# Two adaLN transformer layers: the softmax shifts turned by one transpose, and written by four transfers a unit

## The reference, cut to what matters

```
scores = jnp.einsum('bhqd,bhkd->bhqk', q, k) / jnp.sqrt(jnp.float32(HEAD_DIM))
scores = jnp.where(causal[None, None], scores, -jnp.inf)
attn = jax.nn.softmax(scores, axis=-1)
out = jnp.einsum('bhqk,bhkd->bhqd', attn, v)
```

## Time and profile before

| | us |
|---|---|
| median of 3 runs | 1355.31 (1354.32 to 1356.49) |
| span of the profiled execution | 1351.6 |
| PE busy | 1152.9 |
| DVE busy | 962.7 |
| ACT busy | 695.5 |
| POOL busy | 240.5 |

### The profile page before, as it was taken

One profiled execution on the slowest core, in us unless ns is written; L12 is line 12 of the kernel. 1 busy time (PEld: TensorE's weight loads), 2 busy tenths in 40 slices (PEclk: granted clock), 3 DMA queues, 4 the chain that ended last, 5 costly groups with the idle time before them and its releaser, 6 DMA issues. The chain is left out here.

```text
span 1351.6 us, 39302 instructions
## 1 busy us (share of the span) xinstructions
PE 1152.9 (85%) x16626; PEld 581.8 (43%) x16627; DVE 962.7 (71%) x2700; ACT 695.5 (51%) x929; POOL 240.5 (18%) x271
## 2 busy tenths in 40 slices
PE   5878999999899997297368899999899999778993
PEld 4423434434344444175123343444334454546662
DVE  5888989989698853511558998989788882564553
ACT  4424657666567674142334465766666668323330
POOL 2440000101000000277121000100200000135761
PEclk9678989999899997599678898999999999689997
DMA  4441000503200000221353111330400000011123
GB/s 142 142 80 41 19 19 19 92 19 55 57 3 5 5 3 2 45 54 53 95 154 65 35 37 36 67 65 4 76 3 4 5 4 3 1 40 38 48 47 107
DMA packets 38022, 60.46 MB, mean 45 GB/s; under 512 B 6288, under 2 KB 29104, under 8 KB 36720
## 3 DMA queue, kind: packets, MB, share of 16 engines
q0 software_dynamic: 7648, 24.47, 9.2%
q1 hardware_dynamic: 30208, 33.57, 8.6%
HBM read 42.84 MB, written 14.12 MB: 42 GB/s over the span
## 5 line engine op out<-in xcount | busy, mean ns | idle before, releaser
L978 ACT ACTIVATE probs_at<-st 128x1024 f32<-128x1024 f32 (+3 forms) x640 | 545.1, 897 | 323.2 <-PE st L931 221.1
L996 DVE TENSOR_REDUCE mxp_at<-mx 128x1 f32<-128x512 f32 x768 | 497.3, 685 | 69.1 <-PE mx L898 67.6
L898 PE MATMUL mx<-ks,qs 128*32 128x512 bf16 (+3 forms) x5120 | 390.8, 367 | 40.5 <-DVE mxp_at L996 11.4
L931 PE MATMUL st<-qs,ks 128*32 128x512 bf16 (+3 forms) x5120 | 363.5, 355 | 10.6 <-DMA qs<-shrow_at 8.1
L949 PE MATMUL av<-probs_at,vs 128*32 128x512 f32 (+3 forms) x2560 | 290.9, 530 | 0.3
L898 PEld LDWEIGHTS mx<-ks,qs 128*32 128x32 bf16 x5120 | 137.2, 97 | 344.3 <-DVE mxp_at L996 140.6
L998 DVE CUSTOM_DVE_ANT_0 junk_at<-mx,maskN 128x384 f32<-128x384 f32 (+3 forms) x512 | 240.9, 485 | 39.3 <-PE mx L898 36.2
L931 PEld LDWEIGHTS st<-qs,ks 128*32 128x32 bf16 x5120 | 133.9, 98 | 97.8 <-ACT probs_at L978 22.6
L1274 POOL DMA_INDIRECT taken<-table,token x71 | 68.1, 959 | 251.1 <-DVEq L1063 218.3
L935 PE MATMUL st<-maskTb,identb 128*32 128x128 bf16 x2048 | 103.8, 220 | 0.0
L949 PEld LDWEIGHTS av<-probs_at,vs 128*32 128x32 f32 x2560 | 69.7, 111 | 47.8 <-issue 5.6
(11 more groups left out here) (271 smaller groups left out, 1043.5 us busy)
## 6 DMA issues: line engine op xcount, KB each, us to landing
qs<-q_parts POOLq DMA_DIRECT2D x54, 128.0 KB, 5.7
ks<-k_parts POOLq DMA_DIRECT2D x18, 384.0 KB, 6.7
weights<-in_w_dram SPq DMA_DIRECT2D x16, 256.0 KB, 3.0
table<-rows SPq DMA_DIRECT2D x8, 260.0 KB, 5.4
got_pj<-eo SPq DMA_DIRECT2D x4, 512.0 KB, 5.5
got_cb<-eo SPq DMA_DIRECT2D x4, 512.0 KB, 5.4
weights<-in_dw_dram SPq DMA_DIRECT2D x3, 576.0 KB, 4.9
weights<-in_gw_dram SPq DMA_DIRECT2D x3, 528.0 KB, 3.8
```

The lines of the kernel that those rows point to most:

```text
L898: mm = pe.matmul(buf[z:z + 32, 0:w], QS[p][:, j, (4 * Q + qb) * P + z:(4 * Q + qb) * P + z + 32], KS[p][:, j, c * CH:c * CH + w], start=Tr ...
L931: mm = pe.matmul(st[half][z:z + 32, y, off:CH], KS[p][:, j, kb * P + z:kb * P + z + 32], QS[p][:, j, Q * CH + off:(Q + 1) * CH], start=Tru ...
L978: act.activation(probs[:, s % 2, 2 * half:2 * half + 2, off:CH], st[half][:, :, off:CH], ACT.Exp, scale=SCALE).then_inc(exp_done[half], 1)
L996: ins = v.tensor_reduce(dst, buf[:, 0:w], AX.X, ALU.max)
```

## The change

The four blocks of a unit's shifts are turned by a single transpose, 128x32 to 32x128: row 8 * block + r. The copy takes 32 rows of 128 columns. As the blocks now lie under one another and not side by side, each goes to its place by a transfer of its own, 8 rows x 4 heads x 128 columns; the semaphores count four. The planner's two costs of a turn change with it.

```diff
@@ schedule()
             else:
-                pe += .22
-                dve = max(dve, pe + lat) + .6
+                pe += .06
+                dve = max(dve, pe + lat) + .25
                 ready[x] = dve + 2.4
@@ attention()
-        shrow = sb("shrow", [2 * GH, 4, CH], BF)
+        shrow = sb("shrow", [TPC * 2 * GH, 4, P], BF)
@@ SyncE
                         sp.wait_ge(shift_row, UB + u + 1)
-                        sp.dma_start(QS[g % 2][SHIFT0:SHIFT0 + 2 * GH, :, Q * CH:(Q + 1) * CH],
-                                     shrow[:, u % 4, :].unsqueeze(1).to_broadcast([2 * GH, GH, CH])).then_inc(shift_set[u % 4], 16)
+                        for qb in range(TPC):
+                            b = TPC * Q + qb
+                            sp.dma_start(QS[g % 2][SHIFT0:SHIFT0 + 2 * GH, :, b * P:(b + 1) * P],
+                                         shrow[2 * GH * qb:2 * GH * (qb + 1), u % 4, :].unsqueeze(1).to_broadcast([2 * GH, GH, P])
+                                         ).then_inc(shift_set[u % 4], 16)
@@ GpSimd
-                g.wait_ge(shift_set[0], 16 * (L * (NU // 4) + 1))
+                g.wait_ge(shift_set[0], 16 * TPC * (L * (NU // 4) + 1))
@@ TensorE
                         pe.wait_ge(shift_split, UB + x + 1)
-                        for qb in range(TPC):
-                            mm = pe.transpose(buf[:].bitcast(BF)[0:2 * GH, qb * P:(qb + 1) * P], nsh[:, x % 4, qb, :], m.identb[:])
-                        mm.then_inc(mx_ready, 1)
+                        pe.transpose(buf[:].bitcast(BF)[0:TPC * 2 * GH, 0:P], nsh[:, x % 4].rearrange("p q r -> p (q r)"),
+                                     m.identb[:]).then_inc(mx_ready, 1)
@@
-                            pe.wait_ge(shift_set[u % 4], 16 * (L * (NU // 4) + u // 4 + 1))
+                            pe.wait_ge(shift_set[u % 4], 16 * TPC * (L * (NU // 4) + u // 4 + 1))
@@ VectorE
                         if x >= 4:
-                            v.wait_ge(shift_set[x % 4], 16 * (L * (NU // 4) + x // 4))
-                        v.tensor_copy(shrow[:, x % 4, :], buf[:].bitcast(BF)[0:2 * GH, 0:CH]).then_inc(shift_row, 1)
+                            v.wait_ge(shift_set[x % 4], 16 * TPC * (L * (NU // 4) + x // 4))
+                        v.tensor_copy(shrow[:, x % 4, :], buf[:].bitcast(BF)[0:TPC * 2 * GH, 0:P]).then_inc(shift_row, 1)
```

## The result

The changed kernel takes 1393.7 us (median of 4 runs, 1393.06 to 1395.03) against 1354.8 for the one before beside it: ratio 1.0299, 95% interval 1.0266 to 1.0332. I forecast slower, 1368.6 us, with a range up to 1378: the sign was right, the size a third of the real one. The profiled execution has a span of 1392.5 us against 1351.6, 40.9 more.

A forecast was written before the change was run, and what follows sets the result against it. TensorE and VectorE, handing three PSUM banks to and fro, bound the attention stages. 22.2 us more wait x 0.86 = 19.1 lost, less 5.8 won on the copy: 13.3 us slower, 1368.6 us, range 1354 to 1378.

The forecast's parts named there:

- The copy: VectorE's shift copy on 32x128 takes 0.19 us; 6.8 us of VectorE saved, 5.8 us of time won.
- The issues: SyncE issues each of a unit's four shift transfers in about 0.69 us, the last 2.19 us later than the only one now.
- cheap issues: Rival: back-to-back SyncE issues cost 0.34 us each, as on L739; 2.3 us slower, 1357.6 us; chance 0.18.
- The landing in a quiet queue: At uncontended gates the last shift transfer lands 2.46 us after its issue, which comes 2.19 us later than now.
- the nine: Units without a DMA wait now, scores 2.47 to 3.19 us after the issue; 17.2 us more wait.
- Which gates: Scores of 14 units would wait for shift transfers: nine with little slack and five already waiting.
- The contended five: Units where TensorE already waits for the DMA, 9.9 us together; 5 us more wait, between 0 and 11.0.
- How much arrives: Comparing the two attention layers, 0.86 of a TensorE wait reaches the end; 22.2 us of wait loses 19.1 us.
- the banks that cover the gates: Rival: VectorE's three filled banks, 1.8 us of work, cover TensorE's gate waits; 4 us faster, 1351.5 us; chance 0.1.
- Fixed costs in a row: Rival: each shift transfer lands before the next moves, 7.4 us at each of 14 gates; +81 us, 1436 us; chance 0.02.
- The planner's costs: Turn costs of 0.06 and 0.25, not 0.22 and 0.6, leave gates tight; order elsewhere worth 3 us either way.
- the rival 'order': Rewritten order puts more products ahead of the gates, 6 to 9 us faster, 1347 us, or fewer, slower; chance 0.1.

The follow-up runs named there:

- the two by two: Changed kernel with the planner's old or new turn costs for first/last eight units: old/old 1380.9, new/old 1387.1, old/new 1384.8, new/new 1391.5 us.

## Why the prediction was wrong

- *The copy*: predicted 0.19 us, measured 0.205; DVE busy 954.2 us against 962.7. Right. What it is worth in time was 5.8 us in my sum. Transfers alone came at 1.0179, and transfers with the new copy and transpose at 1.0144 on the same chip, 4.7 us less, and at 1.0192 on another, 1.8 us more, with intervals of 4 or 5 either way. So 5.8 is neither shown nor ruled out.
- *The issues*: predicted 0.69 us each, measured 0.686, the last 2.2 us behind the first. Right; the rival of cheap issues is dead.
- *The landing in a quiet queue*: I had the last transfer take as long as the big one, 2.19 + 2.46 = 4.65 from the first issue. It took 4.09 to the scores. I had the waits of the nine at 17.2 us, and 17.5 is what they came to, but by luck: eight of them took 13.2, where my count gives 15.3, and the ninth, (0,0) of the first layer, took 4.3 alone. Its last transfer goes out 0.28 us behind a transfer of GpSimd's (L863, at 73.31), which in the kernel before is issued 1.9 us behind the only one; whether that is the cause was not tried.
- *Which gates*: 14, as read from the slack. Right.
- *The contended five*: the step "I take 5, a little under the middle, because the worst of the five (7.10) is long enough to swallow the 2.19 and the others hardly" failed, and its upper bound of 11.0 as well: 14.0 us came on. The two gates of (0,1) have 9.5 of it, from 1.3 to 7.1 us in the first layer and from 2.4 to 6.1 in the second. Bounding it by the spacing of the issues, 2.19 each, supposed that the transfers are held up once and as long as the one was; 5.8 and 3.7 us are more than that, and moving the loads away took them back to 1.45 and 1.70. (0,0) of the second layer, the one that I had said would swallow the 2.19, has 3.8 of it, and these can't be put down to the cutting. All gates together: 31.5 us more wait, not 22.2, not all of it for certain by the transfers: the changed kernel waits 41.4 and 40.5 us in its two executions with a profile, with the old order 35.0 and 36.1.
- *How much arrives*: 0.86 predicted, 0.74 measured with the transfers alone. Near enough, given how rough the second is; the banks that cover the gates are dead as a rival. 32.7 x 0.86 = 28 would have been said for the 24.2 us.
- *Fixed costs in a row*: dead, since the last of four transfers was usable 4.09 us behind the first issue and not 9.9. The 2.0 us that the prediction took from the Trainium skill ("DMA: Bandwidth & Descriptors", section "Anatomy of one DMA — SWDGE (gpsimd) path") stand there for transfers that GpSimd issues; these are SyncE's.
- *The planner's costs*: the step "so the gates stay tight. Elsewhere the order may shift; I put 3 us either way" failed. The gates did stay tight, but the order costs 10.6 us in the changed kernel and 8.5 in the one before. I had looked at the distance from copy to gate only, and at the stretches from first to last copy as "all the kernel that the change touches". The end of the stage lies behind them: there cheaper turns move two steps of scores out of cover, 4 us a layer. In the first half one product less ahead of two gates is the side of the rival 'order' that "adds to my figure".
- *The sum*: 24.2 for the transfers and 10.6 for the order are 34.8, less what the copy saves, against 36.9 and 38.9 measured for the whole. The terms have intervals of 4 to 6 us each, so it closes within the measurements. Against my 13.3 us, 25.6 were lacking: 5 by the transfers (24.2, not 19.1), 10.6 by the order, and the 10 that are left belong to no single step; up to 5.8 of them are the copy's saving, if it did not arrive.

## What to carry to other kernels

A transfer on the path of a gate has a price for its count: cutting 32 KB into four cost 1.6 us of landing in a quiet queue and up to 6 where large loads run beside it, against 0.2 us saved on the copy. The spacing of the issues is no upper bound on the landing under load. And costs in a planner are part of the change: giving it truer costs for one item moved work out of cover elsewhere, and only the corners of the two by two, side by side on one chip, told how much. A wait that already swings between kernels, like that of (0,0) in the second layer, must be read in several of them before it is put down to a change.

## What was not expected of the hardware

- A transfer within SBUF of 8 rows x 4 copies is issued by SyncE in 686 ns whether it has 1024 or 256 bytes a piece; the same destination shape from DRAM takes 301 ns.
- With a quarter of the bytes the last transfer landed sooner behind its issue: about 4.09 - 2.19 = 1.9 us against 2.46.
- The kernel with extra products at the gates had its granted clock back at 0.95 and no measurable gain, though the products also held up some of the scores.
- The first scores of (0,0) in the second layer waited from 4.2 to 8.0 us for their shifts, with one transfer as with four.
- The same kernel came out at 1376.0 and 1380.9 us, ratio 1.0144 and 1.0192, on two chips. The intervals overlap, so it may be noise; either way, half a per cent between variants needs them side by side.
